# Products of zeros, split sums and states that cross the array's halves in a recurrence and a long convolution on one core

## The chip, the core and the metric

The kernel runs on one core of a Trainium2 chip. The time is that of one execution on the device in microseconds. Three executions of the kernel before took 978.77, 973.68 and 973.1 us; the median is 973.68.

## The reference, cut to what matters

```python
# x [8, 512, 256], cond_1024 [8, 256], all float32
def cond(x, h0, Wx, Wh, b):              # a recurrence over 512 steps
    xw = einsum('ntd,dh->nth', x, Wx) + b
    step: next_h = tanh(xw_t + prev_h @ Wh)         # batch 8, width 256
def attn(u, A_log, D, C_re, C_im, log_dt):          # a long convolution per channel
    dt = exp(log_dt); A = -exp(A_log)
    K[m, t] = sum_n C_re[m, n] * exp(dt[m] * A[n] * t)          # 64 states
    return irfft(rfft(u) * rfft(K))[:512] + u * D
def cond2(x, h0, W_f, ...):              # normalised gates, cumulative sums in log space
def ffn(x, ...):                         # x + shared expert + top 2 of 16 experts, d_ff 352
x = x + attn(cond(x, cond_1024, ...), ...)
x = x + ffn(cond2(x, cond_1024, ...), ...)
```

Everything in `cond` depends on the step before it; `attn` needs its whole output.

## The kernel before

Each engine has its own instruction list in `build`, and semaphores order them. The stages follow each other: recurrence, transposes, convolution, gates, routing, shared expert, 16 experts. The change touches the first three.

**The recurrence.** `steps` (L520 ff.) runs in a loop of IT = 32 iterations with 2 banks of G = 8 steps; n = 0 to 15 counts the steps in an iteration. The hidden state is kept transposed, 256 rows in C = 2 halves of 128 partitions, 8 columns for the batch. A step has 16 matmuls (`state_product`, L516): output half o, contracted half k, column group j of 32 columns. A float32 matmul is two instructions in the trace, so a step shows 32. ScalarE writes tanh of half 0 and half 1 (L879), and `s_h` releases the next step. Behind its products each step puts work that the next does not need: parts of the input products of the coming 8 steps (`inputs_summed`, L508; by `INPUTS`, one bias unit of 8 instructions in steps t = 1, 3, 5, two units of 16 in all in t = 2, 4, 6 of either bank, the first three units with 64 columns and the others with 32), four products of zeros (`keep_groups_up(192)`, L489) in all steps but n = 7, and in n = 7 the sums for 4 channels of the convolution's kernel (`kernel_sums`, L494). GpSimd turns the states round into `uT` (L418), VectorE writes the kernel's parts out.

**Transposes.** 64 of them (L565) bring the outputs `uT` to rows by time; VectorE (L1160) and ScalarE (L905) copy them to `u_tok`.

**The convolution** works in blocks of HB = 64 steps and in 16 chunks of CP = 8 channel pairs, one channel of the first 128 and one of the last 128, on partitions 0 to 63 and 64 to 127 (k = 0, 1). A chunk m (z = m % 2) is: `own_block` (L590), the block's own part, with a Toeplitz tile; `block_states` (L577) of the next chunk, which forms the 64 states that each block leaves; `carried` (L599), what comes from the states that the blocks before left. VectorE's scan (L1169, `carry`) lets the states decay from block to block, GpSimd prepares the powers' arguments and the decays (L393, L404), ScalarE takes the exponentials (L892) and copies two operands of a later chunk to fixed slots (L897, L902), one DMA a chunk does that for the Toeplitz tile, and VectorE adds the result to `xtok` (L1175). The waits of each part hang on a small product of zeros ahead of it (`stand`, L604).

A matmul's tile position (row, column) says which part of the array it uses. `own_block` and `carried` use all four 64x64 tiles: rows k, columns odd or even block. `block_states` uses the two on the diagonal, (0, 0) and (64, 64). Its outputs go to PSUM bank z.

The functions that the change touches:

Of the kernel before, what the change touches and what calls it, by code (L numbers as in the profile page):

```python
# [53 lines left out]
def build(nc, x_tok, x_steps, h0_gate, wx_d, wh_d, b_rec_d, pack_d,  # L54
# [5 lines left out]
    with ExitStack() as ctx:  # L60
# [10 lines left out]
        sizes = (C * B, NST, 1, P + KP, P, IT, KP * C * KP, 8, HB, RB, R + CT)  # L71
        pack = sb("pack", [P, sum(sizes)])
        h0r, a_bc, a_q, dt_q, c_q, d_k, masks, consts, iota_t, resets_t, rows_to = [pack[:, sum(sizes[:n]):sum(sizes[:n + 1])] for n in range(len(sizes))]
# [158 lines left out]
        s_own = sem("s_own")  # L232
        s_slot_tz = [sem("s_slot_tz0"), sem("s_slot_tz1")]
# [6 lines left out]
        block = ctx.enter_context(nc.Block())  # L240

# [142 lines left out]
        def _(pool):  # L384
# [7 lines left out]
            def power_args(m):  # L392
                pool.tensor_tensor(pw[:, m % 2], dt_q[:, CP * m:CP * m + CP].unsqueeze(2).to_broadcast([P, CP, NST]),  # L393
                                   a_bc.unsqueeze(1).to_broadcast([P, CP, NST]), ALU.mult).then_inc(s_pa, 1)
# [5 lines left out]
            pool.wait_ge(s_dtm, 3)  # L400
            for m in range(2):
                power_args(m)
            def block_decays(m):
                pool.tensor_tensor(d0[:, m % 2], lam[:, CP * m:CP * m + CP].unsqueeze(2).to_broadcast([P, CP, RB]),  # L404
                                   resets_t.unsqueeze(1).to_broadcast([P, CP, RB]), ALU.mult).then_inc(s_d0, 1)
# [72 lines left out]
        def _(pe):  # L478
# [49 lines left out]
            def steps(i, bank):  # L528
                for t in range(G):
# [26 lines left out]

            pe.wait_ge(s_hist, 2 * IT + 2)
            pe.wait_ge(s_kev, IT)
            pe.wait_ge(s_late, LATE)
            for n in range(2 * NB):  # L560
# [5 lines left out]
                last.then_inc(s_utr, 1)  # L566

# [4 lines left out]
            def block_states(z):  # L572

                for c in range(CP):
                    for k in range(C):
                        to = ps[rows_of_half(k), z, RB * c:RB * c + RB].rearrange("p (b t) -> p b t", t=NB)[:, :, 1:NB]
                        last = nc.tensor.matmul(to, pw[rows_of_half(k), z, c], u_tok[rows_of_half(k), CP * z + c].rearrange("p (b t) -> p b t", t=NB)[:, :, 0:NB - 1],  # L577
                                                start=True, stop=True, skip_group_check=True, tile_position=(HB * k, HB * k))
# [15 lines left out]
            def carried(z):  # L594

                for c in range(CP):
                    for k in range(C):
                        for odd in range(2):
                            last = nc.tensor.matmul(to_tokens(z, c, k, odd), qd[rows_of_half(k), CP * z + c], xc[rows_of_half(k), z, c].rearrange("p (r e) -> p r e", e=2)[:, :, odd],  # L599
                                                    start=False, stop=True, skip_group_check=True, tile_position=(HB * k, HB * odd))  # L600
# [11 lines left out]
            with pe.Fori(0, NCH // 2) as i:  # L612
                for z in range(2):
# [248 lines left out]
        def _(act):  # L862
# [6 lines left out]
            nc.scalar.activation(dt_q[:], dt_q[:], ACT.Exp).then_inc(s_dtm, 1)  # L869
            act.wait_ge(s_dta, 1)  # L870
# [621 lines left out]
```

## Time and profile before

| what | value |
|---|---|
| runs | 973.1, 973.68, 978.77 us |
| the profiled execution | 974.19 us, of which the span is 972.3 |
| TensorE busy | 924.3 us (95%), weight loads 777.5 (80%) |
| VectorE, ScalarE, GpSimd busy | 410.7, 506.3, 299.1 us |
| mean granted TensorE clock | 0.978 |
| the chain that ended last | 81% TensorE, 5% issue, 4% ScalarE, 4% GpSimd, 3% VectorE, 2% DMA |

Busy time of TensorE counts matmuls that overlap, so its share says little of how fast it works; what an engine waited for, and how long it is from the start of one part to the start of the next, says more. Instructions of one kind that follow each other are merged in a timeline, with their count behind an x. A clock of 1.00 is 2.4 GHz, one of 0.50 is 1.2 GHz.

### The profile page before, as it was taken

To read this page: it belongs to the slowest core of one execution; us is meant where nothing else is said; L and a number is where in the kernel's file an instruction comes from. 1 tells how busy PE (TensorE), PEld (TensorE's weight loads), DVE (VectorE), ACT (ScalarE), POOL (GpSimd) and SP (SyncE) were. 2 spreads that over 40 slices of the span, in tenths; PEclk is the share of its full clock that TensorE was granted. 3 is DMA by queue.
4 is the path that set the end of the run, shared out by engine and by line. 5 is a ranking of instruction groups with operands and counts; after the bars stand their busy time and mean duration, and the time that the engine had idled before them with its cause. 6 is when DMAs were issued, how large, how long until landed. Compare 5 with 4: busy or idle time off the path is not lost.

```text
span 972.3 us, 64880 instructions
## 1 busy us (share of the span) xinstructions
PE 924.3 (95%) x28864; PEld 777.5 (80%) x28864; DVE 410.7 (42%) x781; ACT 506.3 (52%) x1735; POOL 299.1 (31%) x324
## 2 busy tenths in 40 slices
PE   7999999999999999999999998999899999999993
PEld 5888888888888888996444446788899999999993
DVE  1000010100001103553899799875564646556450
ACT  2444444444444446443876587134465656566551
POOL 3111111111111110650003463760045364554545
PEclk6799999999999999999999999999999999999997
DMA  2222222221111111111001110533357666675634
GB/s 89 83 92 87 95 93 87 100 85 33 35 40 36 35 33 28 66 76 57 0 1 39 49 56 22 184 116 108 127 132 162 133 157 119 151 146 127 134 40 53
DMA packets 69161, 80.34 MB, mean 83 GB/s; under 512 B 24225, under 2 KB 53558, under 8 KB 69122
## 3 DMA queue, kind: packets, MB, share of 16 engines
q1 hardware_dynamic: 54242, 62.18, 20.3%
q0 software_dynamic: 14592, 17.10, 10.7%
q8 instruction: 23, 0.38, 0.2%
q10 hardware_dynamic: 288, 0.56, 0.2%
q14 instruction: 16, 0.13, 0.0%
HBM read 44.16 MB, written 33.83 MB: 80 GB/s over the span
## 4 chain that ended last, share of the span: by engine, by line
PE 81%; issue 5%; ACT 4%; POOL 4%; DVE 3%; DMA 2%; POOLq 0%; SPq 0%; ACTq 0%; DVEq 0%
PE ps L516 19%; PE ps L811 16%; PE ps L508 9%; PE ps L825 8%; PE ps L677 8%; PE ps L489 6%; PE ps L727 3%; POOL slots_in L447 2%; PE ps L577 2%; ACT tok L879 2%; PE ps L590 2%; PE ps L736 2%; PE ps L599 2%; PE ps L494 2%; DMA slots_in<-tok,arena 1%
## 5 line engine op out<-in xcount | busy, mean ns | idle before, releaser
L516 PE MATMUL ps<-tok,wh 128*32 128x8 f32 x16384 | 255.2, 180 | 12.9 <-issue 3.5
L879 ACT ACTIVATE tok<-ps 128x8 f32<-128x8 f32 x1024 | 155.9, 177 | 204.0 <-PE ps L516 201.6
L516 PEld LDWEIGHTS ps<-tok,wh 128*32 128x32 f32 x16384 | 220.0, 113 | 48.0 <-ACT tok L879 25.2
L466 POOL DMA_INDIRECT out<-arena,dest x80 | 127.9, 1599 | 99.3 <-ACT arena L1030 76.9
L489 PE MATMUL ps<-zero 128*32 128x192 bf16 x1920 | 141.1, 255 | 0.0
L418 POOL TENSOR_TENSOR big<-tok,zero 128x128 f32 x64 | 29.0, 453 | 322.0 <-ACT tok L879 322.0
L811 PE MATMUL ps<-xgT_hi,ew_hi 128*128 128x320 f32 (+1 forms) x384 | 119.5, 311 | 3.2 <-DVE spare L1275 1.6
L811 PE MATMUL ps<-xgT_hi,ew_lo 128*128 128x320 f32 (+1 forms) x384 | 119.5, 311 | 0.0
L811 PE MATMUL ps<-xgT_lo,ew_hi 128*128 128x320 f32 (+1 forms) x384 | 119.0, 310 | 0.0
L1143 DVE TENSOR_TENSOR arena<-arena,pack 128x256 f32 x32 | 13.6, 426 | 246.3 <-ACT arena L884 246.3
L1381 DVE TENSOR_TENSOR mid<-mid,ps 128x320 f32<-128x320 f32 (+1 forms) x96 | 46.6, 486 | 107.0 <-ACT mid L1048 57.5
L677 PE MATMUL ps<-mid,gw 128*128 128x512 f32 x192 | 83.8, 593 | 2.5 <-ACT mid L958 1.6
L447 POOL DMA_INDIRECT slots_in<-tok,arena x64 | 73.1, 1142 | 23.6 <-issue 17.1
L1048 ACT ACTIVATE mid<-ps 128x320 f32<-128x320 f32 (+1 forms) x96 | 41.8, 435 | 73.9 <-PE ps L811 71.0
L508 PE MATMUL ps<-xst,wx 128*32 128x64 f32 (+1 forms) x3120 | 76.3, 209 | 0.0
L677 PEld LDWEIGHTS ps<-mid,gw 128*128 128x128 f32 x192 | 36.1, 190 | 46.5 <-issue 45.2
L811 PEld LDWEIGHTS ps<-xgT_hi,ew_hi 128*128 128x128 f32 (+1 forms) x384 | 69.2, 180 | 4.0 <-DVE spare L1275 1.9
L825 PE MATMUL ps<-ew_hi,eact_hi 128*128 128x256 f32 (+1 forms) x240 | 71.7, 299 | 0.3 <-ACT arena L1030 0.3
L489 PEld LDWEIGHTS ps<-zero 128*32 128x32 bf16 x1920 | 62.1, 96 | 11.5 <-issue 0.5
L811 PEld LDWEIGHTS ps<-xgT_lo,ew_hi 128*128 128x128 f32 (+1 forms) x384 | 69.4, 181 | 0.0
L811 PEld LDWEIGHTS ps<-xgT_hi,ew_lo 128*128 128x128 f32 (+1 forms) x384 | 69.3, 180 | 0.0
L825 PE MATMUL ps<-ew_lo,eact_hi 128*128 128x256 f32 (+1 forms) x240 | 67.8, 282 | 0.0
(206 smaller groups left out, 1643.5 us busy)
## 6 DMA issues: line engine op xcount, KB each, us to landing
slots_in<-mid SPq DMA_DIRECT2D x16, 645.0 KB, 3.7
mid<-slots_in SPq DMA_DIRECT2D x16, 645.0 KB, 4.2
arena<-in_ex_down SPq DMA_DIRECT2D x16, 384.0 KB
arena<-in_ex_gate SPq DMA_DIRECT2D x16, 352.0 KB
arena<-in_ex_up SPq DMA_DIRECT2D x16, 352.0 KB
xst<-in_x_steps SPq DMA_DIRECT2D x66, 64.0 KB, 1.8
xtok<-in_x_tok SPq DMA_DIRECT2D x16, 256.0 KB, 2.7
mid<-k_pad SPq DMA_DIRECT2D x32, 128.0 KB, 3.1
```

Of the source, the lines that this page charges most:

```text
L447: pool.indirect_dma_start(out=slots_in[:, :], out_offset=bass.IndirectOffsetOnAxis(ap=idx[:, k, r:r + 1], axis=0), in_=hid_tok[:, r, :], i ...
L466: pool.indirect_dma_start(out=out[:, :], out_offset=bass.IndirectOffsetOnAxis(ap=dest[:, z, t:t + 1], axis=0), in_=yo[:, z, t], in_offset= ...
L489: nc.tensor.matmul(ps[Q * j:Q * j + Q, 6, 0:columns], zero16[:, 0:Q], zero16[:, 0:columns], start=True, stop=True, tile_position=(0, Q * j))
L508: last = nc.tensor.matmul(ps[Q * j:Q * j + Q, to, 0:cols], w, v, start=c < 0, stop=c == C - 1, skip_group_check=True, tile_position=(0, Q ...
L516: last = nc.tensor.matmul(sums_at(bank, t, o)[Q * j:Q * j + Q], wh[:, k, columns(j, o)], hring[:, (n - 1) % (2 * G), k], start=False, stop ...
L677: last = nc.tensor.matmul(ps[:, gate_bank(n % NT, q), :], gw[:, q, c, z * P:(z + 1) * P], x1T[:, c, 4 * b:4 * b + 4, :].rearrange("p r t - ...
L727: last = nc.tensor.matmul(ps[0:fw, bank, :], of(w)[:, c, f0:f0 + fw], v, start=c == 0 and p == 0, stop=c == C - 1 and p == len(parts) - 1)
L811: last = nc.tensor.matmul(ps[0:fw, 2 * h + m % 2, 0:HALF], of(w)[:, c, f0:f0 + fw], v[:, c, hf * HALF:(hf + 1) * HALF], start=c == 0 and p ...
L825: last = nc.tensor.matmul(ps[:, 4 + (z + t) % 2, 0:D], a[0:fw, f, t * P:(t + 1) * P], down_of(w)[0:fw, f], start=f == 0 and p == 0, stop=f ...
L879: nc.scalar.activation(hring[:, n, o], sums_at(n // G, n % G, o), ACT.Tanh).then_inc(s_h[o], 1)
L1048: nc.scalar.activation(esil[0:fw, m % 2], ps[0:fw, m % 2, 0:HALF], ACT.Silu).then_inc(s_esil, 1)
L1381: nc.vector.tensor_tensor(eprod[0:fw, m % 2], esil[0:fw, m % 2], ps[0:fw, 2 + m % 2, 0:HALF], ALU.mult).then_inc(s_eact, 1)
```

## The change

- Recurrence: `keep_groups_up` has 320 columns for 192 and stands only in steps 0, 2, 4, 6, 10, 12 and 14. `kernel_sums` is split, two channels behind n = 7 and two behind n = 8; one wait (`s_ps0`) goes.
- After the loop, 28 products of zeros of 8 columns over the whole array. After the transposes, ten of 256 columns.
- `block_states` sends channels with an odd c across: rows k, columns 1 - k. The set of a chunk spans two banks, even channels in the first 256 columns, odd in the last; `d0`, `xc` and the kernel's masks, `c_q` and `dt_q` follow that order, and a copy `dt_s` in the old order (one more exponential on ScalarE, 128 more columns in the pack) feeds the powers.
- `carried` is split: even channels ahead of `block_states`, odd ones behind it. With that, the waits for the scan and for both slot copies stand ahead of `carried(z, 0)`.
- `stand` is 128 weights by 128 columns added to the result's unused columns, for 32 by 8.

```diff
-        sizes = (C * B, NST, 1, P + KP, P, IT, KP * C * KP, 8, HB, RB, R + CT)
+        sizes = (C * B, NST, 1, P + KP, P, P, IT, KP * C * KP, 8, HB, RB, R + CT)
...
+        def states_at(z):
+            return psf[:, 512 * 6 * z + 256:512 * 6 * z + 768]
+        def place_of(c):
+            return CP // 2 * (c % 2) + c // 2
...
-            def kernel_sums():
-                for c in range(KP):
+            def kernel_sums(half):
+                for c in range(KP // 2 * half, KP // 2 * half + KP // 2):
                     last = nc.tensor.matmul(ps[0:C * KP, 4, 0:HB], cblk[:, c], kq[:, c], start=c == 0, ...)
-                last.then_inc(s_kmm, 1)
+                if half == 1:
+                    last.then_inc(s_kmm, 1)
...
-                    if n != G - 1:
-                        keep_groups_up(192)
+                    if n in (0, 2, 4, 6, 10, 12, 14):
+                        keep_groups_up(320)
                     if n == G - 1:
-                        pe.wait_ge(s_ps0, 1)
                         pe.wait_ge(s_kqe, i + 1)
                         pe.wait_ge(s_kc, i + 1)
-                        kernel_sums()
+                        kernel_sums(0)
+                    if n == G:
+                        kernel_sums(1)
...
+            for _ in range(28):
+                keep_up(8)
             pe.wait_ge(s_hist, 2 * IT + 2)
...
+            pe.wait_ge(s_xc, 1)
+            for _ in range(5):
+                nc.tensor.matmul(ps[:, 0, 0:256], zero16[:, 0:P], zero16[:, 0:256], start=True, stop=True)
+                nc.tensor.matmul(ps[:, 0, 0:256], zero16[:, 0:P], zero16[:, 0:256], start=True, stop=True)
...
-                        to = ps[rows_of_half(k), z, RB * c:RB * c + RB].rearrange(...)[:, :, 1:NB]
+                        h, at = k ^ c % 2, RB * place_of(c)
+                        to = states_at(z)[rows_of_half(h), at:at + RB].rearrange(...)[:, :, 1:NB]
...
-                                                start=True, stop=True, skip_group_check=True, tile_position=(HB * k, HB * k))
+                                                start=True, stop=True, skip_group_check=True, tile_position=(HB * k, HB * h))
...
-            def carried(z):
-                for c in range(CP):
-                    for k in range(C):
+            def carried(z, crossed):
+                for c in range(crossed, CP, 2):
+                    for h in range(C):
                         for odd in range(2):
...
-                last.then_inc(s_qmm, 1)
-            def stand():
-                nc.tensor.matmul(ps[0:Q, 6, 0:B], zero16[:, 0:Q], zero16[:, 0:B], start=True, stop=True, tile_position=(0, 0))
+                last.then_inc((s_half, s_qmm)[crossed], 1)
+            def stand(z):
+                at = R * CP
+                nc.tensor.matmul(ps[:, 2 + 2 * z, at:at + P], zero16[:, 0:P], zero16[:, 0:P], start=False, stop=False, skip_group_check=True)
...
-                    stand()
+                    stand(z)
                     own_block(z)
+                    pe.wait_ge(s_xc, m + 2)
                     pe.wait_ge(s_pe, m + 2)
-                    pe.wait_ge(s_xc, m + 1)
                     pe.wait_ge(s_uea, 2 * m + SLOTS - 1)
-                    stand()
+                    stand(z)
+                    carried(z, 0)
                     block_states(1 - z)
-                    pe.wait_ge(s_xc, m + 2)
-                    pe.wait_ge(s_uea, 2 * m + SLOTS - 2)
-                    stand()
-                    carried(z)
+                    pe.wait_ge(s_half, m + 1)
+                    stand(z)
+                    carried(z, 1)
...
+            nc.scalar.activation(dt_s[:], dt_s[:], ACT.Exp).then_inc(s_dtm, 1)
...
-            nc.vector.memset(ps[:, 0:2].rearrange("p n (c t) -> p (n c) t", t=NB)[:, :, 0], 0.0).then_inc(s_xc, 1)
+            nc.vector.memset(ps[:, 0:2].rearrange("p n (c t) -> p (n c) t", t=NB)[:, :, 0], 0.0)
+            dve.wait_ge(s_utr, 1)
+            nc.vector.memset(ps[:, 6:8].rearrange("p n (c t) -> p (n c) t", t=NB)[:, :, 0], 0.0).then_inc(s_xc, 1)
```

## Rows read from the trace of the kernel before

**Rows 1.** Chain that ended last, shares of the span by line.

```profile
PE ps L516 19%; PE ps L811 16%; PE ps L508 9%; PE ps L825 8%; PE ps L677 8%; PE ps L489 6%; PE ps L727 3%; POOL slots_in L447 2%; PE ps L577 2%; ACT tok L879 2%; PE ps L590 2%; PE ps L736 2%; PE ps L599 2%; PE ps L494 2%; DMA slots_in<-tok,arena 1%
```

**Rows 2.** Stretch: length, busy us (instructions) PE, PEld, DVE, ACT, POOL; clock, DMA.

```profile
7.76:35.07 27.31, 22.52 (x1049) 20.29 (x1050) 1.32 (x5) 8.07 (x50) 3.56 (x6) 0.50 0.16 55
35.07:378.30 343.23, 333.95 (x22086) 285.51 (x22083) 32.48 (x122) 160.49 (x1034) 45.47 (x92) 1.00 0.22 67
...
388.18:447.84 59.66, 58.37 (x2640) 54.57 (x2640) 29.50 (x31) 27.48 (x44) 29.41 (x28) 1.00 0.17 62
```

**Rows 3.** Timeline of ScalarE: start us, length us, instruction. Starts of the tanh.

```profile
193.57 0.30 ACT L879 ACTIVATE tok<-ps 128x8 f32<-128x8 f32 x2 [0.53 <-PE ps L516]
194.24 0.30 ACT L879 ACTIVATE tok<-ps 128x8 f32<-128x8 f32 x2 [0.37 <-PE ps L516]
194.98 0.30 ACT L879 ACTIVATE tok<-ps 128x8 f32<-128x8 f32 x2 [0.44 <-PE ps L516]
195.66 0.30 ACT L879 ACTIVATE tok<-ps 128x8 f32<-128x8 f32 x2 [0.37 <-PE ps L516]
196.35 0.30 ACT L879 ACTIVATE tok<-ps 128x8 f32<-128x8 f32 x2 [0.39 <-PE ps L516]
...
199.20 0.30 ACT L879 ACTIVATE tok<-ps 128x8 f32<-128x8 f32 x2 [0.51 <-PE ps L516]
...
204.02 0.30 ACT L879 ACTIVATE tok<-ps 128x8 f32<-128x8 f32 x2 [0.37 <-PE ps L516]
204.85 0.30 ACT L879 ACTIVATE tok<-ps 128x8 f32<-128x8 f32 x2 [0.53 <-PE ps L516]
```

**Rows 4.** Timeline of TensorE, same columns: behind n=9 and n=10.

```profile
194.23 0.31 PE L508 MATMUL ps<-spare,brow 1*32 1x64 f32 x8
194.47 0.27 PE L489 MATMUL ps<-zero 128*32 128x192 bf16 x4
194.57 0.43 PE L516 MATMUL ps<-tok,wh 128*32 128x8 f32 x32
...
195.10 0.27 PE L489 MATMUL ps<-zero 128*32 128x192 bf16 x4
195.21 0.50 PE L516 MATMUL ps<-tok,wh 128*32 128x8 f32 x32
```

**Rows 5.** Timeline of TensorE: kernel_sums behind n=7, then n=8.

```profile
203.99 0.55 PE L494 MATMUL ps<-arena 128*8 128x64 f32 x7
...
204.38 0.46 PE L516 MATMUL ps<-tok,wh 128*32 128x8 f32 x27
```

**Rows 6.** ScalarE in the second iteration, and stretches as in rows 2.

```profile
28.24 0.38 ACT L879 ACTIVATE tok<-ps 128x8 f32<-128x8 f32 x2 [0.54 <-PE ps L516]
...
34.73 0.30 ACT L879 ACTIVATE tok<-ps 128x8 f32<-128x8 f32 x2 [0.50 <-PE ps L516]
...
386.64:390.05 3.41, 2.25 (x85) 2.01 (x84) 1.59 (x3) 1.93 (x3) 0.58 (x1) 1.00 0.00 0
690.43:693.84 3.41, 1.49 (x9) 1.28 (x10) 3.41 (x6) 0.63 (x2) 0.00 (x0) 1.00 0.00 0
...
693.84:697.25 3.41, 3.41 (x15) 3.41 (x14) 0.55 (x2) 0.44 (x1) 0.00 (x0) 0.50 0.57 192
```

**Rows 7.** Timeline of all engines: behind the loop, behind the transposes.

```profile
379.38 7.64 PE L565 MATMUL ps<-ident,big 128*128 128x128 f32 x64 [0.91 <-POOL big L418]
...
388.18 1.14 PE L577 MATMUL ps<-tok,arena 64*64 64x56 f32 x32 [1.16 <-DVE tok L1160]
```

**Rows 8.** The chain in the chunks (start, length, what), and VectorE's scan.

```profile
389.43 1.06 PE ps L590 x64
...
390.60 1.07 PE ps L577 x32
...
391.72 1.22 DVE L1169 TENSOR_TENSOR_SCAN arena<-arena,ps 128x512 f32<-128x512 f32 x1 [1.09 <-PE ps L577]
```

**Rows 9.** DMA issues: what, size, us from issue to landing.

```profile
pack<-in_pack ACTq DMA_DIRECT2D x1, 289.0 KB, 3.0
```

More of the change, by code:

```diff
@@ L70, in build @@
         h0g = sb("h0g", [P, C, B])
-        sizes = (C * B, NST, 1, P + KP, P, IT, KP * C * KP, 8, HB, RB, R + CT)
+        sizes = (C * B, NST, 1, P + KP, P, P, IT, KP * C * KP, 8, HB, RB, R + CT)
         pack = sb("pack", [P, sum(sizes)])
-        h0r, a_bc, a_q, dt_q, c_q, d_k, masks, consts, iota_t, resets_t, rows_to = [pack[:, sum(sizes[:n]):sum(sizes[:n + 1])] for n in range(len(sizes))]
+        h0r, a_bc, a_q, dt_q, dt_s, c_q, d_k, masks, consts, iota_t, resets_t, rows_to = [pack[:, sum(sizes[:n]):sum(sizes[:n + 1])] for n in range(len(sizes))]
         h0r = h0r.rearrange("p (c b) -> p c b", c=C)
@@ L232, in build @@
         s_own = sem("s_own")
+        s_half = sem("s_half")
         s_slot_tz = [sem("s_slot_tz0"), sem("s_slot_tz1")]
@@ L392, in power_args @@
             def power_args(m):
-                pool.tensor_tensor(pw[:, m % 2], dt_q[:, CP * m:CP * m + CP].unsqueeze(2).to_broadcast([P, CP, NST]),
+                pool.tensor_tensor(pw[:, m % 2], dt_s[:, CP * m:CP * m + CP].unsqueeze(2).to_broadcast([P, CP, NST]),
                                    a_bc.unsqueeze(1).to_broadcast([P, CP, NST]), ALU.mult).then_inc(s_pa, 1)
@@ L592, in own_block @@
                 last.then_inc(s_own, 1)
[L594 to L597 removed]
+            def carried(z, crossed):
+                for c in range(crossed, CP, 2):
+                    for h in range(C):
                         for odd in range(2):
[L599 to L604 removed]
+                            last = nc.tensor.matmul(to_tokens(z, c, h ^ crossed, odd), qd[rows_of_half(h), CP * z + c], xc[rows_of_half(h), z, place_of(c)].rearrange("p (r e) -> p r e", e=2)[:, :, odd],
+                                                    start=False, stop=True, skip_group_check=True, tile_position=(HB * h, HB * odd))
+                last.then_inc((s_half, s_qmm)[crossed], 1)
+            def stand(z):
+                at = R * CP
+                nc.tensor.matmul(ps[:, 2 + 2 * z, at:at + P], zero16[:, 0:P], zero16[:, 0:P], start=False, stop=False, skip_group_check=True)
             pe.wait_ge(s_uev, NB)
@@ L1168, in carry @@
                 z = m % 2
-                nc.vector.tensor_tensor_scan(xc[:, z].rearrange("p c r -> p (c r)"), d0[:, z].rearrange("p c r -> p (c r)"), ps[:, z, :], 0.0, ALU.mult, ALU.add).then_inc(s_xc, 1)
+                nc.vector.tensor_tensor_scan(xc[:, z].rearrange("p c r -> p (c r)"), d0[:, z].rearrange("p c r -> p (c r)"), states_at(z), 0.0, ALU.mult, ALU.add).then_inc(s_xc, 1)
             def add_x(m):
@@ L1446, with crossed @@
     masks = np.zeros((P, KP, C, KP), f32)
-    masks[:, np.arange(KP), :, np.arange(KP)] = (half[:, None] == np.arange(C))[None]
+    masks[:, np.arange(KP), :, np.arange(KP)] = (half ^ np.arange(KP)[:, None] % 2)[:, :, None] == np.arange(C)
     over = np.zeros((P, KP), f32)
+    def crossed(v):
+        w = v.reshape(C, P, -1).copy()
+        w[:, 1::2] = w[::-1, 1::2]
+        return w
     steps = x.reshape(B, S // G, G // 2, 2, C, P).transpose(1, 5, 4, 3, 2, 0).reshape(S // G, P, C, G, B)
@@ L1457 @@
     tri = np.stack([np.triu(np.ones((P, P)), 1) - 1, np.ones((P, P))], 1).astype(f32)
-    pack = (rows(cond.T), np.broadcast_to(a_log, (P, NST)), np.tile(a_log, C), np.concatenate([np.repeat(dt.reshape(C, P), HB, 0), over], 1),
-            c_re.reshape(C, P, NST).transpose(0, 2, 1), d_k, masks, consts, np.broadcast_to(-np.arange(HB, dtype=f32), (P, HB)),
+    pack = (rows(cond.T), np.broadcast_to(a_log, (P, NST)), np.tile(a_log, C), np.concatenate([np.repeat(crossed(dt)[:, :, 0], HB, 0), over], 1), np.repeat(dt.reshape(C, P), HB, 0),
+            crossed(c_re).transpose(0, 2, 1), d_k, masks, consts, np.broadcast_to(-np.arange(HB, dtype=f32), (P, HB)),
             np.broadcast_to((np.arange(RB) % NB > 0).astype(f32), (P, RB)),
```

9 lines of the change are left out of this document (5 added, 4 removed).

## The prediction

> **What bounds the kernel now.** I read the chain of work that ended last first. It is TensorE nearly everywhere, and the recurrence's own lines (L516, L508, L489) hold a third of it [rows 1]. Then the stretches: after a slow start the recurrence runs from 35.07 to 378.30 us at the full clock with TensorE busy 334.0 of 343.2 us, and the convolution's chunks from 388.18 to 447.84 us with TensorE busy 58.4 of 59.7, while VectorE, ScalarE and GpSimd are busy half of that [rows 2]. Only these stretches are touched, so what counts is TensorE's order there.
>
> One step of the recurrence is a circle: TensorE's 32 products, the tanh of the first half, and back. The starts of the tanh show how long each step takes [rows 3]. From n=8 at 193.57 us the steps take 0.67 (n=9), 0.74 (n=10), 0.68 (n=11), 0.69 (n=12), and from n=7 at 204.02 to n=8 0.83. 0.67 us is the floor that the circle sets: products start 0.23 us after the tanh before them at the earliest (195.21 - 194.98) and their own tanh starts 0.44 later [rows 3, 4]. A step longer than that is one in which TensorE still had something queued [rows 4]: behind n=9 the eight bias products take 0.24 us, the four products of zeros 0.10, and n=10 starts at 194.57 instead of 194.24 + 0.23 = 194.47. Behind n=7 kernel_sums puts eight products of 0.05 each on one column group, and the bulk of n=8 starts at 204.38, 0.13 after 204.02 + 0.23 [rows 3, 5]. The steps n=1 to n=6 have the same inputs as n=9 to n=14, so one half of an iteration stands for both.
>
> **The recurrence, part by part.** The change takes the four products of zeros out of steps 1, 3, 5, 8, 9, 11, 13 and 15, widens them from 192 to 320 columns in the seven others (step 7 had none), and puts half of kernel_sums behind n=8.
> - n=2 and n=10: without 0.10 of zeros ahead of them both start on time: 2 x 0.07 = 0.14 us an iteration.
> - n=4, 6, 12, 14: 0.69 becomes 0.67 (narrower bias products ahead of them): 4 x 0.02 = 0.08.
> - n=8: half of the sums is 0.22 and ends before the tanh comes back: 0.16. The other half lies behind n=8, which has no inputs and no zeros any more. What waits for the sums (GpSimd's next arguments, VectorE's copy, the store of the kernel) gets them one step later and has some eight steps of room.
> - n=3 and n=11: behind the 64-column inputs the zeros end just as the next step may start (195.10 + 0.10, next start 195.21, [rows 4]). 128 more columns at 2.4 GHz are 0.05 us, of which I let 0.03 vanish in what the neighbouring step gains, so +0.02 each, +0.04. In the other steps with 320 columns the inputs are narrower or absent and the 0.05 is hidden by the wait for the tanh.
>
> Together 0.14 + 0.08 + 0.16 - 0.04 = 0.34 us an iteration, 32 iterations: **-10.9 us**. Bounds: 0 if each of the seven wider groups delays by its 0.05 (7 x 0.05 = 0.35), -13 if none does and the jump to the next iteration gains too.
>
> **The chunks.** A chunk is now own_block with 64 products in 1.06 us, block_states with 32 in 1.07, carried with 64 that repeat own_block's row, and a carrier of waits ahead of each, 0.11 (390.60 - 389.43 - 1.06, [rows 8]). So a state product takes 33 ns and the others 17. In both, however, one 64x64 tile has 16 products in 1.06 us, 66 ns each: block_states uses two tiles of the array, the others four. The change sends the odd channels across (rows k, columns 1-k), so four tiles take eight each: 8 x 66 = 0.53 us. That is 0.53 saved, 16 chunks and one ahead of the loop: **-9.0 us**. Bounds: 0, if two tiles are not the limit; -10.9 at the 13.4 ns of the recurrence's products (32 in 0.43, [rows 4]).
>
> The 48 carriers get 128 columns and 128x128 weights for 8 columns and 128x32: 120 columns more are 0.05 us, 96 more columns of weights up to 0.04 when not hidden. 0 to 0.09 each; I take 0.07, as the next products want the part of the array that it holds: **+3.4 us** (0 to 4.3).
>
> The wait for the scan moves forward, ahead of carried(z, 0) and so ahead of block_states. What is queued behind it is all of TensorE. The scan starts when the states' products end and takes 1.22 [rows 8]: about 0.65 + 1.22 + 0.06 = 1.93 us after block_states began. TensorE comes to the wait after 0.53 (states), 0.17, 0.53 (carried, odd channels), 0.17, 1.06 (own) = 2.46. It is hidden with 0.5 to spare. Next late would be VectorE: 29.5 us over 16 chunks is 1.8 each, and GpSimd, 29.4 over 14, is 2.1 [rows 2], against a new chunk of 1.06 + 2 x 0.53 + 0.53 + 3 x 0.18 = 3.2 us, from 3.7. The slot DMAs keep more than one chunk between the products that free a slot and those that read it. The wait for s_half is on products that ended 0.5 us before.
>
> **Edges.** Behind the loop 28 small products with 128x128 weights go into a gap of 0.91 us of idle time, 1.1 from issue to issue [rows 7]. No row shows them. Low end 13.4 ns each, 0.4 us, hidden; high end 119 ns, a transpose's share of 7.64/64 [rows 7], +2.3 us. Nearest is a turn on one tile, 66 ns, as each must wait for the one before: 1.85 - 1.1 = **+0.8 us**. After the transposes ten products of 256 columns, 1.07 us at 2.4 GHz, go into 1.16 us [rows 7]: 0, up to +0.5. The second memset stands on VectorE ahead of its copies: +0.1 (0 to 0.2). The pack grows from 289 to 353 KB and 3.0 us to landing [rows 9]; in proportion +0.7, but the first step waited for other inputs until 2 us later: **+0.1**. The added Exp of dt_s lies on ScalarE while TensorE still sums inputs: 0.
>
> **The sum.** -10.9 - 9.0 + 3.4 + 0.8 + 0.1 + 0.1 = -15.5 us. The profiled execution took 974.19 us, its span is 972.3 and 1.9 lies around it. 974.2 - 15.5 = 958.7. It was 0.5 above the median of 973.68, so 958 us.
>
> **Rivals.**
> 1. Two tiles are not what makes a state product 33 ns; the shared bank is. For: own_block's two row halves write different banks and run at 17 ns, block_states' both write bank z. The new order still puts both halves of a channel in one bank and alternates only from channel to channel; of each four products three would remain at 33 ns and one fall to 17, (3 x 33 + 17)/4 = 29 ns, 0.93 us a set, 2.4 us in all instead of 9.0. Against: the equal 66 ns per tile, though 56 and 32 columns stream. Time 958 + 6.6 = 964.5. In the Trainium skill, "TensorEngine Tiling (Array Packing)", Gotcha 1 says that different row tiles cannot access the same PSUM bank simultaneously; no run here shows it yet, and by it this rival would be the result. Chance 0.14.
> 2. The wider zeros cost what the dropped ones gave, 0.05 at each of the seven steps. For: n=11 was already exactly on time [rows 4]. Against: behind n=8 the zeros stood too and n=9 came at the floor, so where there are few inputs or none they are covered. 958 + 10.9 = 969. Chance 0.13.
> 3. Slower: TensorE's clock falls during the recurrence. At the low level n=0 to n=7 took 34.73 - 28.24 = 6.49 us, at the full one 204.02 - 199.20 = 4.82 [rows 3, 6]: 35% more, 3.9 us an iteration of 11.28 (204.85 - 193.57). A stretch at 1.2 GHz like the one from 693.84 to 697.25 us [rows 6] would cost 3.41 x (1 - 1/1.35) = 0.9. With one in each iteration: 958 + 32 x 0.9 = 987. It is slower than before from about 18 such falls, and the whole recurrence at the low level would add 119. For: from 7.76 us on the clock was low for 27 us although TensorE was busy for 22.5 of them [rows 2], and the new steps 7 to 9 and 15 have no zeros. Against: it stayed full with TensorE busy 2.25 of 3.41 us at 386.64 and fell only behind a stretch with 1.49 [rows 6]; the steps that lose their zeros, but for 9 and 15, are those in which TensorE has bias products or sums and is hardly idle. Chance 0.10.
>
> **How the numbers follow.** My forecast has 0.58; 0.05 is for more than I sum (hidden carriers, an earlier rise of the clock), below 949. A measurement here tells about 1%, 9.7 us, from no change, so faster means below 964. The forecast's own range is 950 to 963. Rival 1 sits on the bound, a third of it below; rival 2 is no change, rival 3 slower. Faster 0.58 + 0.05 + 0.05 = 0.68; same 0.21; slower 0.11. The range takes in rivals 1 and 2 and the bounds of the small terms: 949 to 972.
>
> **What would show it.** Steps n=2 and n=8 at 0.67 to 0.69 between tanh starts, an iteration of about 10.9 for 11.28 us; n=3 at 0.69. 32 state products in 0.53 us, not 0.93. Carriers 0.16 to 0.2 from start to next. TensorE not idle ahead of carried(z, 0). The first transpose at most 0.8 later after the last tanh. The clock at 1.00 from the second iteration to the end of the chunks. The forecast is wrong if the clock shows falls between 40 and 370 us, if state products stay near 30 ns, or if the even steps grow by 0.05.

## The result and the profile after

| | runs, us | median |
|---|---|---|
| before | 978.77, 973.68, 973.1, 974.13 | 973.9 |
| after | 993.6, 993.49, 992.33, 993.91 | 993.55 |

The ratio is 1.018 (95% interval 1.0148 to 1.0216): 19.6 us slower, where 16 faster was forecast. The profiled execution took 993.6 us, its span is 991.8, 19.5 more than before. One thing has to be known for all numbers below: in some executions of either kernel TensorE's clock falls in the convolution and the execution is some 30 to 40 us longer; the ratios below leave such executions out where a kernel has both kinds, and where that hides the matter I give the counts.

The page of the kernel after: the busy share of TensorE in 40 slices, the clock in tenths, the chain.

```profile
PE   7999999999999999999999999999899999999993
PEclk6799999999999997555999999999999999999997
PE ps L527 21%; PE ps L832 16%; PE ps L519 8%; PE ps L846 8%; PE ps L698 8%; PE ps L499 4%; PE ps L618 3%; PE ps L609 3%; PE ps L748 3%; POOL slots_in L457 3%; PE ps L757 2%; PE ps L504 2%; PE ps L596 1%; PE ps L625 1%; DMA slots_in<-tok,arena 1%
```

The clock has a hole of 7, 5, 5, 5 at slices 16 to 19, which are the convolution and the start of the gates. TensorE is busy at 9 there all the same, and the chain [rows 1] looks almost as before. Stretches of the kernel after, cut where the stages and the clock change (columns as in rows 2):

```profile
35.00:366.00 331.00, 324.33 (x21072) 270.20 (x21069) 27.06 (x122) 160.56 (x1034) 46.32 (x91) 1.00 0.22 69
366.00:375.99 9.99, 9.69 (x106) 9.11 (x103) 7.71 (x10) 8.70 (x12) 0.45 (x1) 1.00 0.08 19
375.99:383.12 7.13, 5.94 (x289) 5.22 (x293) 3.02 (x3) 3.35 (x6) 4.20 (x4) 1.00 0.11 39
383.12:462.79 79.67, 79.14 (x2364) 70.46 (x2357) 26.77 (x28) 24.57 (x39) 25.23 (x24) 0.50 0.12 43
462.79:471.86 9.07, 7.51 (x19) 3.97 (x16) 0.69 (x1) 1.19 (x2) 0.00 (x0) 0.50 0.37 123
471.86:991.80 519.94, 490.87 (x2898) 403.35 (x2897) 335.40 (x605) 298.39 (x587) 216.97 (x188) 0.99 0.40 96
```

Against [rows 2]: the recurrence ends 12.3 us earlier. The clock then falls at 383.12, in the second of the 16 chunks, to 1.2 GHz, and stays there for 88.7 us; in the first 79.67 of them TensorE is busy for 79.14. ScalarE's tanh in the recurrence (start, length, as in rows 3): n=10 and n=11, then n=15 and n=0, n=7 and n=8, n=15 and n=0 of the next iteration, and the last one:

```profile
199.17 0.30 ACT L901 ACTIVATE tok<-ps 128x8 f32<-128x8 f32 x2 [0.37 <-PE ps L527]
199.85 0.30 ACT L901 ACTIVATE tok<-ps 128x8 f32<-128x8 f32 x2 [0.37 <-PE ps L527]
...
202.53 0.30 ACT L901 ACTIVATE tok<-ps 128x8 f32<-128x8 f32 x2 [0.37 <-PE ps L527]
203.25 0.30 ACT L901 ACTIVATE tok<-ps 128x8 f32<-128x8 f32 x2 [0.41 <-PE ps L527]
...
207.95 0.30 ACT L901 ACTIVATE tok<-ps 128x8 f32<-128x8 f32 x2 [0.37 <-PE ps L527]
208.62 0.30 ACT L901 ACTIVATE tok<-ps 128x8 f32<-128x8 f32 x2 [0.37 <-PE ps L527]
...
213.33 0.30 ACT L901 ACTIVATE tok<-ps 128x8 f32<-128x8 f32 x2 [0.37 <-PE ps L527]
214.10 0.30 ACT L901 ACTIVATE tok<-ps 128x8 f32<-128x8 f32 x2 [0.47 <-PE ps L527]
...
366.00 0.30 ACT L901 ACTIVATE tok<-ps 128x8 f32<-128x8 f32 x2 [0.37 <-PE ps L527]
```

Nearly every wait for the products is now 0.37 us and nearly every step 0.67 [rows 3 has up to 0.83]; the step across the loop's end takes 0.72 and 0.77 here. TensorE from the end of that loop into the chunks:

```profile
366.00 0.85 PE L494 MATMUL ps<-zero 128*128 128x8 bf16 x28
367.06 1.16 PE L579 MATMUL ps<-ident,big 128*128 128x128 f32 x8 [0.22 <-POOL big L428]
...
375.99 0.69 PE L596 MATMUL ps<-tok,arena 64*64 64x56 f32 x32
376.61 0.23 PE L625 MATMUL ps<-zero 128*128 128x128 bf16 x1
376.77 1.14 PE L609 MATMUL ps<-tok,mid 64*64 64x32 f32 x64
378.15 0.23 PE L625 MATMUL ps<-zero 128*128 128x128 bf16 x1 [0.24 <-DVE arena L1193]
378.31 0.67 PE L618 MATMUL ps<-arena 64*64 64x32 f32 x32
378.80 0.67 PE L596 MATMUL ps<-tok,arena 64*64 64x56 f32 x32
379.40 0.23 PE L625 MATMUL ps<-zero 128*128 128x128 bf16 x1
379.56 0.67 PE L618 MATMUL ps<-arena 64*64 64x32 f32 x32
380.16 0.23 PE L625 MATMUL ps<-zero 128*128 128x128 bf16 x1
380.32 0.67 PE L609 MATMUL ps<-tok,mid 64*64 64x32 f32 x32
381.93 0.67 PE L609 MATMUL ps<-tok,mid 64*64 64x32 f32 x32 [0.94 <-issue]
```

The 28 zeros lie in the old gap, transposes and first states start 12.3 and 12.2 us earlier than in [rows 7], and 32 state products take 0.60 us from their start to the next start (378.80 to 379.40), where rows 8 have 1.07. So what was costed works. The last line is new: in the middle of own_block, whose 64 products wait for nothing from each other, TensorE stands for 0.94 us, "issue": no semaphore, no other engine. Before had this too, shorter (TensorE, the kernel before, same columns):

```profile
393.90 0.65 PE L590 MATMUL ps<-tok,mid 64*64 64x32 f32 x26 [0.23 <-issue]
```

The trace's DMA records point to code that is late. In them the queue that carries instructions brings 16 KB at a time (23 such packets in the execution, 0.38 MB). The DMA view of the kernel after, window 378.9 to 379.2 us, has one of them (packets, MB, share of the engines):

```profile
q8 instruction: 1, 0.02, 29.4%
```

It starts at 379.12 us and takes 1.41, and 1.40 after its end, at 381.93, TensorE goes on. The same holds in all profiles below: each stop over 0.3 us in the first pass of the chunks' loop, behind the loop's first product, ends 1.3 to 1.6 us after the end of such a packet. In the first pass of the recurrence's loop in the kernel before, six come 3.7 to 3.9 us apart (8.28, 12.04, 15.73, 19.62, 23.53, 27.19). Later passes of that loop fetch nothing, and in the later passes of the chunks' loop of the kernel after there is one packet (at 408.5), beside which TensorE doesn't stop. In its first pass the loop over the chunks needs such blocks too, and the new chunk gets through its instructions sooner.

The balance: -12.2 to the start of the first states. From there to the last add into xtok (L1199, at 462.90) 86.9 us against 59.7 [rows 2], +27.3. The rest, +4.4, lies behind, where the gates begin at 1.2 GHz. Together 19.5. The 27.3 are a difference of two things: the same stage took 55.6 us in g_slot0 below, where the clock held (374.74 to 430.33), so the new chunks save 4.1 and the fall costs 31.3.

### The profile page after: what moved, and what is told of

It reads as the page before. It is cut to its first block, busy times and chain, and to the rows that moved or that the text cites. A ratio compares the mean times of both kernels' runs of the same rounds, so it can differ in the third digit from the quotient of the medians.

```text
span 991.8 us, 62894 instructions
## 1 busy us (share of the span) xinstructions
PE 945.4 (95%) x27878; PEld 785.0 (79%) x27878; DVE 405.6 (41%) x782; ACT 507.5 (51%) x1736; POOL 301.8 (30%) x324
## 4 chain that ended last, share of the span: by engine, by line
PE 83%; issue 4%; POOL 4%; ACT 3%; DVE 3%; DMA 2%; POOLq 0%; SPq 0%; ACTq 0%; DVEq 0%
PE ps L527 21%; PE ps L832 16%; PE ps L519 8%; PE ps L846 8%; PE ps L698 8%; PE ps L499 4%; PE ps L618 3%; PE ps L609 3%; PE ps L748 3%; POOL slots_in L457 3%; PE ps L757 2%; PE ps L504 2%; PE ps L596 1%; PE ps L625 1%; DMA slots_in<-tok,arena 1%
## 5 line engine op out<-in xcount | busy, mean ns | idle before, releaser
L527 PE MATMUL ps<-tok,wh 128*32 128x8 f32 x16384 | 263.4, 181 | 10.2 <-ACT tok L901 5.7
L698 PE MATMUL ps<-mid,gw 128*128 128x512 f32 x192 | 86.5, 609 | 2.4 <-ACT mid L980 1.6
L499 PE MATMUL ps<-zero 128*32 128x320 bf16 x896 | 83.7, 309 | 0.0
L457 POOL DMA_INDIRECT slots_in<-tok,arena x64 | 75.7, 1182 | 23.7 <-issue 17.1
L519 PE MATMUL ps<-xst,wx 128*32 128x64 f32 (+1 forms) x3120 | 78.7, 208 | 1.0 <-issue 1.0
L846 PE MATMUL ps<-ew_hi,eact_lo 128*128 128x256 f32 (+1 forms) x240 | 67.8, 283 | 0.0
```

The source lines that it names most:

```text
L457: pool.indirect_dma_start(out=slots_in[:, :], out_offset=bass.IndirectOffsetOnAxis(ap=idx[:, k, r:r + 1], axis=0), in_=hid_tok[:, r, :], i ...
L499: nc.tensor.matmul(ps[Q * j:Q * j + Q, 6, 0:columns], zero16[:, 0:Q], zero16[:, 0:columns], start=True, stop=True, tile_position=(0, Q * j))
L519: last = nc.tensor.matmul(ps[Q * j:Q * j + Q, to, 0:cols], w, v, start=c < 0, stop=c == C - 1, skip_group_check=True, tile_position=(0, Q ...
L527: last = nc.tensor.matmul(sums_at(bank, t, o)[Q * j:Q * j + Q], wh[:, k, columns(j, o)], hring[:, (n - 1) % (2 * G), k], start=False, stop ...
L698: last = nc.tensor.matmul(ps[:, gate_bank(n % NT, q), :], gw[:, q, c, z * P:(z + 1) * P], x1T[:, c, 4 * b:4 * b + 4, :].rearrange("p r t - ...
L846: last = nc.tensor.matmul(ps[:, 4 + (z + t) % 2, 0:D], a[0:fw, f, t * P:(t + 1) * P], down_of(w)[0:fw, f], start=f == 0 and p == 0, stop=f ...
```

## The experiments

**First: which part brings it?** The recurrence's part alone in the old kernel, the rest alone, and the whole change with ten dense products of zeros in every second chunk at two places.

```diff
 e1_recurrence = before, with the recurrence's hunks of the change only
 e2_chunks     = after, with the recurrence of before and without the 28 and the ten zeros
 e3 and e4     = after, and
+            def dense(z, times):
+                for _ in range(times):
+                    nc.tensor.matmul(ps[:, 2 + 2 * z, 256:512], zero16[:, 0:P], zero16[:, 0:256], start=False, stop=False, ...)
 e3:                 own_block(z)
+                    if z == 0: dense(z, 10)
 e4:
+                    if z == 1: dense(z, 10)
                     carried(z, 1)
```

> The kernel before with the recurrence's part alone (320 columns of zeros in seven steps, split sums); chunks, carriers and edges as before. Both theories of the clock's fall in the chunks expect the same here, since the old chunks keep it: every step but the loop's jump at 0.67 us, an iteration at 10.9 instead of 11.28 us, the clock full from about 35 us to the end of the chunks, and 974 - 12 = 962 us. If the recurrence's lean zeros were what weakens the clock later, it would fall here too, near the chunks, and the time would be above 974.

> The kernel after with the recurrence of before (192 columns of zeros in 15 steps, sums in one piece) and without the two groups of zeros at the edges; crossed states, split carried and wide carriers stay. Theory 1 (a stop of about 0.9 us of TensorE in the first pass of the chunks' loop lets the clock fall, because the faster chunks reach the code load sooner): a stop of 0.6 to 1.0 us in the first pass, clock at 1.2 GHz for the rest of the loop, 86 us for the chunks, about 974 + 27 + 4 = 1005. Theory 2 (the new chunks are too thin for the clock whatever the first pass does): the same time, with a fall anywhere in the loop. Rival: it is the recurrence's lean zeros or the edges; then the clock stays and the time is 974 - 7 = 967.

> The kernel after with ten products of zeros of 256 columns behind own_block in the even chunks, ahead of the place of the stop in the loop's first pass. In time 8 x 1.07 = 8.6 us of work at the full clock. Theory 1: while these run the code arrives, the stop of 0.94 us shrinks to under 0.3, the clock stays and the time is 993.6 - 27.6 - 4 + 8.6 = 970. Theory 2: the clock stays too, as the loop has more work in it everywhere. So the pair with the next kernel tells them apart: the same work behind the stop.

> The kernel after with the same ten products of zeros of 256 columns, but in the odd chunks, ahead of carried(z, 1): behind the place of the stop. Theory 1: the stop stays at 0.9 us and the clock falls behind it as in the kernel after; it may rise again from the added work, and the time is 980 to 1005. Theory 2: the clock stays as in the kernel with the zeros ahead, 970.

| | runs, us | clock fell for long | ratio |
|---|---|---|---|
| e1_recurrence | 998.63, 1006.14, 962.0, 1002.3 | 3 of 4 | |
| e2_chunks | 1006.3, 1008.3, 1005.18, 1005.63 | 4 of 4 | 1.030 (1.026 to 1.0346) |
| e3_dense_ahead | median 971.5 of 10 | none | 0.994 (0.9912 to 0.9974) |
| e4_dense_behind | median 970.1 of 9 | none | 0.993 (0.9909 to 0.9953) |

e1 is the surprise. It has the old chunks, and its clock falls too. TensorE of e1_recurrence in the first pass, then a stretch behind it:

```profile
381.00 0.32 PE L579 MATMUL ps<-tok,arena 64*64 64x56 f32 x3
382.46 1.14 PE L579 MATMUL ps<-tok,arena 64*64 64x56 f32 x29 [1.14 <-issue]
```

```profile
400.00:460.00 60.00, 60.00 (x1643) 57.14 (x1640) 19.13 (x20) 18.94 (x30) 18.89 (x18) 0.50 0.12 44
```

The clock fell at 383.24, behind a stop of 1.14 us. Its one run without a fall, 962.0, is what the recurrence's part gives: -12, or -14 against the kernel before on the same chip. So either part alone brings falls, and neither is needed for them. The kernel before takes the longer time as well: of its 73 executions in all batches 13 took 1012 to 1015 us, the others 972 to 982; none of the 13 is in a profile, but their mean clock is as low (0.93 to 0.95) as that of the runs that fell. e2 had no stop in the first pass, but without the zeros it waited 1.37 us for VectorE ahead of the first states, and fell at 391.45. e3 and e4 bear out what the hole costs: they are 22 to 23.5 us faster than after though their dense products add some 8.8 (eight passes with ten of 0.11), 31 us in all. e3 shows how. It had stops of 0.59 and 1.31 us, fell at 392.4 and rose after 3.4 (stretches, e3_dense_ahead):

```profile
392.40:395.90 3.50, 3.50 (x71) 2.76 (x73) 0.00 (x0) 0.56 (x1) 0.00 (x0) 0.51 0.20 75
396.00:440.00 44.00, 43.62 (x1954) 38.23 (x1947) 21.63 (x24) 21.76 (x35) 23.15 (x22) 1.00 0.17 66
```

**Second: does the place of the code decide?** The same work, with the loop moved on or back in the instruction list by other counts of zeros ahead of it; the kernel after again; and four dense products for ten.

```diff
 f1_shift_on:  40 zeros of 64 columns for the ten of 256 behind the transposes
 f2_shift_back: for _ in range(7): keep_up(256)       (for range(28): keep_up(8))
 f4_dense_four: if z == 1: dense(z, 4)   ahead of carried(z, 1)
```

> The kernel after once more, as it is, for its spread beside the next two. Theory 1 (the stop of 0.9 us in the first pass of the chunks' loop, a wait for code, lets the clock fall): in each execution the fall, 992 to 994 us, unless the stop is shorter in one. Theory 3 (the stop is the same each time, but whether the clock falls behind it is a matter of when it comes, as 5 of 19 executions of the kernel before came out at 1014 us and the others at 973 to 980): both 993 and about 956 occur.

> The kernel after with the ten products of zeros of 256 columns behind the transposes as 40 of 64 columns: the same 1.1 us of work, 60 instructions more ahead of the loop, so the 16-KB pieces in which TensorE's code arrives are cut elsewhere in the loop. Loop, carriers and products are untouched. Theory 1: the stop in the first pass moves and changes its length; where it falls under 0.4 us the clock stays and the time is 993.6 - 27.6 - 4 - 7 = 955; where it stays near 0.9 or grows, 993. Theory 2 (the new chunks are too thin for the clock): 993 whatever the stop does.

> The kernel after with the 28 products of 8 columns behind the recurrence's loop as seven of 256: the same 0.75 us of work, 42 instructions fewer ahead of the chunks' loop. Theory 1: as in the kernel with 60 more, the stop moves; 955 if it is short, 993 if it is long. Theory 2: 993.

> The kernel after with four products of zeros of 256 columns (0.43 us) ahead of carried(z, 1) in the odd chunks, where ten kept the clock at 970 us. If that much added work still keeps the clock, 8 x 6 x 0.107 = 5.1 us less than 970, 965 us, a version that is faster than both kernels; if not, 997 and the fall back.

| | runs, us | fell | ratio |
|---|---|---|---|
| f3_after_again | 989.76, 990.26, 996.83, 992.89, 989.79, 992.57 | 6 of 6 | 1.016 (1.0134 to 1.019) |
| f1_shift_on | 992.61, 989.45, 995.42, 991.37 | 4 of 4 | 1.016 (1.0134 to 1.0194) |
| f2_shift_back | 995.74, 995.45, 959.86, 996.84 | 3 of 4 | |
| f4_dense_four | 998.08, 961.04, 1000.47, 1000.45, 997.6, 997.54 | 5 of 6 | |

The stops move: f1 had one of 1.10 us, f2 one of 0.97, f4 1.18 and 0.70, and the kernel after itself, profiled again, 0.63 and 1.07. All fell, at 388.8, 386.0, 388.1 and 386.7. The kernel after had 0.94 us and a short stop of 0.37 at first, so the stops of the same code differ from one execution to the next. Four dense products a pass don't bring the clock back, ten do. The odd runs matter most: f2 at 959.86 and f4 at 961.04 have the new chunks with a clock that held. The theory that the new chunks are simply too thin for the full clock, whatever stands ahead of them, falls with these.

**Third: the place set outright.** The head of the loop at instruction 0, 64, 128 or 192 of a block of 256 (a packet of 16 KB), nothing else changed. That 256 instructions make a packet the trace shows too: between the two stops of g_slot0 lie 126 matmuls with as many weight loads, between those of g_slot64 128.

```diff
-            with pe.Fori(0, NCH // 2) as i:
+            with nc.Fori(0, NCH // 2, engines=type(mybir.ALL_ENGINES)([pe.engine]), head_slot={pe.engine: 0}) as i:     # 64, 128, 192; h4: 16
```

> The kernel after with its chunks' loop on TensorE set to begin at instruction 0 of a block of 256 instructions (16 KB); nothing else is changed. Theory 1 (the clock falls behind a stop for code in the loop's first pass, and how long the stop is depends on where the blocks are cut): the body of some 680 instructions crosses two borders in place of three, so one stop at most, 0.3 to 0.6 us; if it stays under 0.5 the clock holds and the time is 955 to 960. Theory 2 (the new chunks are too thin for the clock): 990 to 1000 at any position.

> The same with the loop beginning at instruction 64 of a block: the first border comes 64 instructions sooner, still two in the body. Theory 1: one stop, at another place than with 0 and of another length; 955 to 960 if under 0.5 us, 990 to 997 if near 1. Theory 2: 990 to 1000.

> The same with the loop beginning at instruction 128: three borders in the body of 680 instructions, two of them less than a load of code (about 2.5 us from its start to the end of the stop) apart. Theory 1: two stops, the longer near 1 us, 990 to 997 in most executions. Theory 2: 990 to 1000.

> The same with the loop beginning at instruction 192: three borders. The first comes during the first chunk's own_block, so the code behind it is asked for early. Theory 1: two stops of 0.3 to 1.2 us; the time follows the longer one, 990 to 997 if it is near 1. Theory 2: 990 to 1000.

| loop at | runs, us | fell | ratio |
|---|---|---|---|
| 0 | 956.83, 961.81, 996.95, 961.97, 961.8 | 1 of 5 | 0.983 (0.9761 to 0.9904) |
| 64 | 990.72, 994.46, 994.93, 989.37 | 4 of 4 | 1.015 (1.0079 to 1.0221) |
| 128 | 991.17, 995.65, 995.64, 994.48 | 4 of 4 | 1.017 (1.0122 to 1.0225) |
| 192 | 990.55, 991.2, 993.02, 989.98 | 4 of 4 | 1.013 (1.0078 to 1.019) |

The place alone is worth 29 to 33 us between the medians, on one chip. g_slot0 is the change as it was meant. A chunk of it in TensorE's timeline:

```profile
397.55 1.14 PE L609 MATMUL ps<-tok,mid 64*64 64x32 f32 x64
...
398.77 0.67 PE L618 MATMUL ps<-arena 64*64 64x32 f32 x32
399.26 0.67 PE L596 MATMUL ps<-tok,arena 64*64 64x56 f32 x32
399.86 0.23 PE L625 MATMUL ps<-zero 128*128 128x128 bf16 x1
400.02 0.67 PE L618 MATMUL ps<-arena 64*64 64x32 f32 x32
...
400.78 0.94 PE L609 MATMUL ps<-tok,mid 64*64 64x32 f32 x49
```

3.23 us from own_block to own_block. A chunk of the kernel before takes 3.53:

```profile
404.42 1.14 PE L590 MATMUL ps<-tok,mid 64*64 64x32 f32 x64
...
407.95 1.14 PE L590 MATMUL ps<-tok,mid 64*64 64x32 f32 x64
```

A chunk of the kernel after with the clock down, from block_states to block_states:

```profile
400.59 1.10 PE L596 MATMUL ps<-tok,arena 64*64 64x56 f32 x32
...
403.07 1.94 PE L609 MATMUL ps<-tok,mid 64*64 64x32 f32 x64
...
406.04 0.77 PE L596 MATMUL ps<-tok,arena 64*64 64x56 f32 x19
```

5.45 us, without a gap. But slot 0 doesn't do away with the stops (TensorE of g_slot0, first pass):

```profile
378.54 0.33 PE L596 MATMUL ps<-tok,arena 64*64 64x56 f32 x5 [0.31 <-issue]
...
382.48 0.36 PE L618 MATMUL ps<-arena 64*64 64x32 f32 x10 [0.99 <-issue]
```

The clock held behind 0.99 us here and fell behind a single stop of 0.56 in slot 192 (TensorE of g_slot192, and the stretch behind its fall at 379.65):

```profile
379.31 0.31 PE L618 MATMUL ps<-arena 64*64 64x32 f32 x6 [0.56 <-issue]
```

```profile
379.70:400.00 20.30, 20.30 (x619) 18.35 (x618) 6.40 (x7) 7.46 (x12) 7.04 (x7) 0.50 0.14 53
```

So the length of the stop alone doesn't decide. e4 had one of 0.90 and held, and in f4 nothing followed the 1.18 us until a second stop of 0.70 had come.

**Fourth: is 0 a good place in general?** The kernel before at 0 and at 128, four dense products at 0, and the kernel after at 16.

> The kernel before with its chunks' loop on TensorE begun at instruction 0 of a block; all else as before. Theory A (the fall belongs to the loop's first pass on code that is still being loaded, in the old loop too, and where the blocks are cut sets how often it comes): the old kernel falls in about 9 of 41 executions; here either none (974 us in each) or nearly all (1014). Theory B (the new chunks alone fall at bad positions; the old ones fall at random): about a fifth to a quarter at 1014, as before.

> The kernel before with that loop begun at instruction 128, where the new loop fell in every execution. Theory A: another rate of falls than at 0, up to all of them at 1014 us. Theory B: about a fifth to a quarter at 1014.

> The kernel after with the loop begun at instruction 0 and four products of zeros of 256 columns ahead of carried(z, 1) in the odd chunks. 8 x 0.43 = 3.4 us more than the 957 to 962 of the loop at 0 alone, for a fall in fewer executions than 1 in 5: 961 to 965, each execution faster than before. If position alone decides, the zeros only cost.

> The kernel after with the loop begun at instruction 16. If the place of the borders decides by which products stand between the stop and the next dense work, 16 instructions change little: stops of 0.3 and 1.0 us as at 0, no fall in most executions, 957 to 962. If 0 held by luck of timing, falls in about half of the executions.

| | runs, us | fell |
|---|---|---|
| h1_before_slot0 | 1015.63, 1012.85, 1012.04, 1011.86 | 4 of 4, ratio 1.038 (1.0352 to 1.0406) |
| h2_before_slot128 | 978.3 in the middle of 11, four of them 1009 to 1016 | 4 of 11, ratio of the rest 1.001 (0.9985 to 1.0038) |
| h3_slot0_dense_four | 969.7 to 971.1 three times, 999.5 to 1006 seven times | 7 of 10 |
| h4_slot16 | 989.72, 957.84, 996.16, 993.89 | 3 of 4 |

It is not: h3 and h4 were expected to hold the clock and mostly didn't. The old kernel, whose own place lets it fall in 13 of 73 (3 of 21 on this chip), falls every time at 0 (behind a stop of 0.9 in block_states). The 4 of 11 at 128 are too few to tell from that. At the same place the faster chunk stands longer in its stops, by one profile each: 0.31 + 0.99 us in g_slot0 for 0.87 in h1, and 0.79 + 1.25 in g_slot128 for 0.21 + 0.83 in h2.

h3 says more than its count. TensorE of h3_slot0_dense_four, first pass:

```profile
380.84 0.33 PE L596 MATMUL ps<-tok,arena 64*64 64x56 f32 x5 [0.63 <-issue]
...
384.78 0.53 PE L618 MATMUL ps<-arena 64*64 64x32 f32 x10 [0.99 <-issue]
```

The stops stand at the same products as in g_slot0, with 5 and 10 left, and the clock fell at 383.81, before the first dense product had run (386.22). Up to there the loop is g_slot0's, instruction for instruction. What differed was the chip, the packet ahead of the first stop (1.37 us for 0.93) and with it the stop (0.63 for 0.31). So this fall can't be laid on the four products; the other six of h3 have no profile. And the 1 of 5 of g_slot0 is no rate to count on: each batch ran on a chip of its own, and only counts within a batch compare places. What makes one packet slower than another isn't shown. One execution of h2 took 1576.07 us; nothing that I have explains it, and it stays out of the argument.

**Fifth: take the long stop away.** A small inner loop of dense products ahead of own_block in the odd chunk: four passes of three products in the first pass of the outer loop, one in every later one. It repeats 12 products out of few instructions, so that TensorE works while the next block comes, and costs little later.

```diff
                     stand(z)
+                    if z == 1:
+                        with pe.Fori(i * 4, 4): dense(z, 3)        # k3: i * 8, 8 and dense(z, 2)
                     own_block(z)
```

> The kernel after with the chunks' loop begun at instruction 0 and, ahead of own_block in the odd chunks, a small inner loop of three products of zeros of 256 columns that runs four times in the first pass and once in each later one: 12 + 7 x 3 = 33 products, 3.5 us, and 8 to 11 jumps of some 0.15 us. In the first pass they give 1.3 us of dense work while the next block of code is on its way, so the stop of 1.0 us that stood at the end of that block shrinks under 0.3. If stops in the first pass are what the clock falls behind, each execution holds it: 957 + 3.5 + 1.5 = 962. If it is the thin work alone, falls in some executions, 997.

> The same with two products a pass, eight passes at first: 16 + 14 = 30 products, 3.2 us, more of it (1.7 us and eight jumps) in the first pass. The stop should be gone whichever way the load falls. 957 + 3.2 + 2 = 962, with no falls if stops are the cause; 997 in some executions if not.

| | runs, us | fell | ratio |
|---|---|---|---|
| k1_inner | 958.48, 962.55, 960.87, 960.25 | 0 of 4 | 0.9865 (0.9842 to 0.9888) |
| k3_inner_two_by_eight | 959.06, 960.37, 960.75, 968.84, 969.53, 964.03 | 0 of 6 | 0.990 (0.9865 to 0.9936) |

TensorE of k1_inner, first pass of the chunks, and the whole stage as one stretch:

```profile
378.59 0.33 PE L596 MATMUL ps<-tok,arena 64*64 64x56 f32 x5 [0.33 <-issue]
...
379.68 1.49 PE L630 MATMUL ps<-zero 128*128 128x256 bf16 x12
381.09 1.14 PE L609 MATMUL ps<-tok,mid 64*64 64x32 f32 x64
...
382.32 0.67 PE L618 MATMUL ps<-arena 64*64 64x32 f32 x32
```

```profile
374.70:430.00 55.30, 54.17 (x2541) 46.85 (x2543) 28.00 (x31) 27.99 (x44) 29.42 (x28) 1.00 0.18 68
```

The stop of 0.99 us is gone: L618 runs through with 32 products where g_slot0 stood in it, and the view of the waits names none for issue in this stage but 0.33 and 0.26 (375.74). The zeros took 1.41 us from their start to that of own_block in place of the 0.99, and the other passes pay some 0.4 each. k1_inner has a median of 960.6 us against 974.1 of the kernel before on the same chip, 33 less than the kernel after, and is the fastest version that was not disturbed in any run. Ten executions of two kernels without a fall stand beside 1 in 5 of g_slot0 and 7 in 10 of h3, whose code is the same up to the inner loop. But neither of those nor the kernel after ran on this chip, so that the inner loop, and not the place or the chip, holds the clock is likely and not proved. Nor is it separated whether it helps by covering the second stop or by its dense work right behind the first.

## Why the prediction was wrong, point by point

- **Recurrence, -10.9.** Right, a little small: the last tanh is at 366.00 instead of 378.31, -12.3, and e1's run with a clock that held is 12 to 14 below the kernel before. An iteration takes 10.85 (203.25 to 214.10) for 11.28. Beyond the forecast, n=3 and n=11 hardly grow (n=11 at 0.68: the 320 columns fit into the 0.37 us of waiting), and n=8 gave its full 0.16 (0.67 for 0.83). The jump to the next iteration scatters, 0.68 to 0.84 us for 0.71 to 0.84 before, and gains 0.01 on average. Rival 2 is refuted: its 0.05 at seven steps is not there.
- **States, -9.0.** Right: 0.60 us a set for 1.07, 0.47 saved for 0.53 forecast. Rival 1, 0.93 us a set, is refuted. The rule in the Trainium skill, "TensorEngine Tiling (Array Packing)", Gotcha 1, would have given that. The trace doesn't bear it out: both row halves of a channel write one bank, and the 32 products still took 0.60 us over four tiles.
- **Carriers, +3.4.** 0.16 us for 0.11, +0.05 each, 2.4 in all.
- **The wait for the scan.** Hidden as argued, but for 0.24 us once, in the first chunk, where own_block alone covers it. A chunk takes 3.23 us, forecast 3.2; before it took 3.53, and the 3.7 of the prediction is the whole stage divided by 16.
- **Edges, +1.0.** The 28 zeros took 0.85 us, 0.03 each for the 0.066 that I took, and cost nothing: from the last tanh to the first transpose are 1.06 us, before 1.07. From there to the first states 8.93 for 8.80.
- **The sum** is -12.3 - 8.0 (17 x 0.47) + 2.4 + 0.2 + 0.1 = -17.6 us, forecast -15.5. g_slot0's profiled span is 955.0 for 972.3, -17.3, and the runs of g_slot0, f2 and h4 in which the clock held took 957 to 962 us, where 958 was forecast.
- **The clock.** This step failed: "The clock at 1.00 from the second iteration to the end of the chunks". I put the only fall into the recurrence (rival 3), where each iteration brings dense work back, and priced it at 0.9 us apiece. It came in the chunks, where nothing brings it back: one fall there costs 31 us, and 4 in the gates, which turns a saving of some 17 us into a loss of 19.5. TensorE busy 58.37 of 59.66 us in the chunks [rows 2] looked safe to me, though the one fall that I had seen, at 693.84, came behind a stretch in which TensorE had mostly waited [rows 6]. What I never costed is a wait for code. I took the chunk as a sum of its parts from steady passes and not what its first pass does, where the stop grew from 0.23 us to 0.94. How much of that comes from the shorter chunk and how much from code that now lies elsewhere isn't separated: at the same place the new chunks stop longer (h1 and h2), but the old ones had 1.14 us in e1.
- **What is shown and what is not.** Shown: the loss is the clock in the chunks (e3, e4, g_slot0); the code's place alone moves the median between 962 and 995 (g) and makes the old kernel fall every time (h1); the loss isn't tied to the new chunks (e1, h1) nor to either part of the change. Argued from the traces only: that the stop in the first pass sets off the fall. One ends 0.3 to 3.0 us ahead of each profiled fall in the chunks' first passes but e2's, where the wait was for VectorE, and k1 and k3, which covered one, didn't fall. Open: what exactly the clock reacts to, as 0.99 us passed in g_slot0 and 0.56 did not in slot 192, and why the same code falls in one execution and not in the next. The runs that held in f2, f4 and h4 have no profile, so whether their stops were shorter is not known.

## What to carry to other kernels

Look at the first pass of a long unrolled loop by itself: a wait marked "issue" in the middle of independent products is late code, at the same place it was longer with the faster work in two pairs here, and instructions added or removed ahead move it. Price a fall of the clock by what follows it, the whole rest of a stage of small products, and not by one stretch. Where such a stop lies ahead of a stage of small tiles, a few dense products repeated by a short inner loop in the first pass are worth a try (no fall in ten executions here, and the stage 2.4 us longer than in g_slot0), and the gain of the change has then to be judged with all executions in view, not by the median of four.

## What the runs showed of the hardware

- A packet of the instruction queue is 16 KB and takes 0.9 to 1.8 us over all profiles. In the first pass of the recurrence's loop of the kernel before they come 3.7 to 3.9 us apart, and TensorE's stops in the chunks' first pass end 1.3 to 1.6 us after the end of one (1.40 at 381.93 in the kernel after, 1.44 and 1.48 at 378.54 and 382.48 in g_slot0). With the same code a packet of 0.93 us was followed by a stop of 0.31 (g_slot0), one of 1.37 by 0.63 (h3).
- At 1.2 GHz with 64x64 tiles and float32, TensorE was busy 79.14 of 79.67 us in the kernel after, and the clock stayed low for 82 to 96 us in every profiled execution in which it fell early in the chunks without ten dense products. With ten of 256 columns in each pass of two chunks it was back after 3.4 (e3).
- A chunk takes 5.45 us at the low clock and 3.23 at the full one, 1.69 times, where the steps of the recurrence take 1.35 times as long [rows 3, 6].
- Products of 8 columns with 128x128 weights in bf16 follow each other in 0.03 us (28 in 0.85), less than half of the turn of one 64x64 tile with float32, which is 0.066 us in own_block (16 a tile in 1.06) and 0.075 in the new block_states (8 in 0.60).
